# Three operand buffers instead of four in a transformer block's attention: each group's load is issued later

## What is computed

```python
x = x + layernorm(attn(layernorm(x), w_attn, w_proj, adapter_wte, gating))
x = x + layernorm(ffn(layernorm(x), W_gate, W_up, W_down))

# attn: B, T, C = 2, 1024, 512; 32 heads of 16; rotary q and k
q, k, v = split(x @ w_attn.T)
y = softmax(mask(rope(q) @ rope(k).T / 4)) @ v                # causal, 1024 keys
y = y + gating * softmax(q @ adapter_k.T / sqrt(512)) @ adapter_v  # 10 keys
return y @ w_proj.T
# ffn: (silu(x @ W_gate.T) * (x @ W_up.T)) @ W_down.T, width 1376
```

## Time and profile before

| | |
|---|---|
| median of 3 runs | 1271.32 us (1270.86 to 1271.98) |
| the profiled execution, its own time | 1268.47 us |
| its span, first to last instruction | 1266.8 us |
| TensorE busy | 1124.6 us (89%) |
| VectorE busy | 715.8 us (57%) |
| ScalarE busy | 515.2 us (41%) |
| GpSimd busy | 267.5 us (21%) |
| mean granted TensorE clock | 0.932 |
| attention, first maxima matmul to last product | about 232 to 753 us |

### The profile page before, as it was taken

How to read it: one execution, slowest core, us unless ns; L and a number is a source line. 1 busy time by engine, 2 the same in 40 slices (tenths; PEclk the granted TensorE clock), 3 DMA queues, 4 the chain that set the end, 5 groups by cost and what they waited for, 6 DMA issues and landing times. The chain is left out here.

```text
span 1266.8 us, 18587 instructions
## 1 busy us (share of the span) xinstructions
PE 1124.6 (89%) x7036; PEld 766.5 (61%) x7036; DVE 715.8 (57%) x955; ACT 515.2 (41%) x1058; POOL 267.5 (21%) x260
## 2 busy tenths in 40 slices
PE   3999798778999999999999885774999999999996
PEld 1887686433555555555555334663887887887884
DVE  4856645567788788788787015993224324324324
ACT  3224132233777777777777643432111112111111
POOL 3624526300221111112121102662001001001001
PEclk9999998766999999999999777887999999999998
DMA  6356546523444544444440017873000200200200
GB/s 235 104 156 177 132 129 175 122 58 68 77 100 92 96 89 86 78 77 78 79 84 19 21 36 221 282 234 124 1 1 17 84 1 20 82 1 30 70 1 34
DMA packets 82522, 113.10 MB, mean 89 GB/s; under 512 B 24964, under 2 KB 42500, under 8 KB 82436
## 3 DMA queue, kind: packets, MB, share of 16 engines
q1 hardware_dynamic: 80612, 108.22, 33.2%
q10 hardware_dynamic: 1824, 3.70, 1.5%
HBM read 68.83 MB, written 42.21 MB: 88 GB/s over the span
## 5 line engine op out<-in xcount | busy, mean ns | idle before, releaser
L780 ACT ACTIVATE prob<-ps_s 128x512 f32<-128x512 f32 (+3 forms) x768 | 323.2, 496 | 174.1 <-PE ps_s L890 167.2
L802 DVE TENSOR_REDUCE neg<-ps_m 128x2 f32<-128x1024 f32 (+2 forms) x224 | 248.1, 1146 | 66.4 <-PE ps_m L855 37.3
L890 PE MATMUL ps_s<-q_op,k_op 50*128 50x512 f32 (+2 forms) x768 | 248.3, 455 | 26.1 <-ACT prob L780 13.5
L890 PEld LDWEIGHTS ps_s<-q_op,k_op 50*128 50x128 f32 x768 | 121.2, 195 | 130.3 <-ACT prob L780 60.8
L855 PE MATMUL ps_m<-k_op,q_op 48*128 48x512 f32 (+2 forms) x768 | 185.4, 421 | 11.3 <-DVE neg L802 8.3
L755 POOL TENSOR_SCALAR_AFFINE_SELECT prob<-prob 128x512 f32<-128x512 f32 x128 | 81.2, 634 | 432.9 <-ACT prob L780 432.8
L904 PE MATMUL ps_y<-prob,vg 128*17 128x512 f32 (+3 forms) x1536 | 154.8, 524 | 0.0
L1301 DVE TENSOR_TENSOR hf<-sl,ps_u 128x512 f32<-128x512 f32 (+1 forms) x44 | 30.2, 686 | 187.6 <-PE ps_u L74 187.6
L802 DVE TENSOR_REDUCE neg_far<-ps_m 128x4 f32<-128x512 f32 (+2 forms) x96 | 100.4, 1048 | 31.6 <-PE ps_m L860 30.1
L1370 PE MATMUL ps_d<-w_ffn_high,wp_high 128*128 128x512 f32 (+1 forms) x352 | 115.6, 391 | 0.0
L855 PEld LDWEIGHTS ps_m<-k_op,q_op 48*128 48x128 f32 x768 | 96.8, 198 | 30.0 <-DVE neg L802 22.7
(11 more groups left out here) (161 smaller groups left out, 1757.9 us busy)
## 6 DMA issues: line engine op xcount, KB each, us to landing
raw<-in_w_ffn SPq DMA_DIRECT2D x16, 520.0 KB, 5.8
y_heads<-y_sb SPq DMA_DIRECT2D x32, 256.0 KB, 2.1
k_op<-k_parts SPq DMA_DIRECT2D x28, 256.0 KB, 4.4
q_op<-q_parts SPq DMA_DIRECT2D x56, 128.0 KB, 4.9
v_groups<-v_out SPq DMA_DIRECT2D x16, 272.0 KB, 4.0
x<-in_x SPq DMA_DIRECT2D x4, 1024.0 KB, 7.6
q_parts<-part_h SPq DMA_DIRECT2D x16, 256.0 KB, 2.9
q_parts<-part_l SPq DMA_DIRECT2D x16, 256.0 KB, 2.9
```

What stands on the lines that cost most here:

```text
L780: act.activation(prob[:, v % NPROB, h, unit_cols(u)], ps_s[:, y % NS, unit_cols(u)], ACT.Exp, scale=D ** -0.5).then_inc(s_exp, 1)
L802: nc.vector.tensor_reduce(to[:, :, pairs[0]:pairs[-1] + 1, i - TT * c], scores, axis=AX.X, op=ALU.max, negate=True).then_inc(a_read, 1)
L890: nc.tensor.matmul(ps_s[:, y % NS, lo:BLK], k_op[buf][r, pair, j * P:(j + 1) * P], q_op[buf][r, c, pair, lo:BLK], start=True, stop=True)\
```

## The change

One buffer is given up (NBUF is 3), the one on `wqk_l`, with its `vg`. Since group n + 3 now goes into the buffer of group n, a load can be issued only one group later than before: `load(n + NBUF - 1)` is now `load(n + 2)`, in the same place of SyncE's order, and it is left out for n = 0, because group 2 has been loaded ahead of the loop. What it waits for is still the products of group n - 1. GpSimd writes the ones of three buffers instead of four.

```diff
-NBUF = 4
+NBUF = 3
...
-    for i, name in enumerate(("x", "wqk_h", "wqk_l")):
+    for i, name in enumerate(("x", "wqk_h")):
...
         for n in range(NG):
             if n:
                 store_y(n - 1, 1)
-            if n + NBUF - 1 < NG:
+            if n and n + NBUF - 1 < NG:
                 load(n + NBUF - 1)
```

## The result

The changed kernel takes 1434.5 us (four runs, 1432.2 to 1437.5), the kernel before 1271.1 beside it: ratio 1.129, 95% interval 1.126 to 1.131. It is 163 us slower; the forecast was 133, range 1360 to 1440. The span went from 1266.8 to 1430.4 us.

A forecast was written before the change was run, and what follows sets the result against it. TensorE bounds the kernel, busy 27.42 of 28.43 us per attention group. 13 x (5.4 stall - 0.4 won back + 5.2 half clock) = 133 us on 1268.47 gives 1401, plus 2.85: 1404 us, range 1360 to 1440.

The forecast's parts named there:

- The issue, the landing, and the demand 7.85 us behind the store: Load's last DMA issued 6.0 us after the store, landing 6.9 later; TensorE's chunk 0 wants it at 7.85.
- The stall: TensorE waits for the load at chunk 0, 5.4 us (3.7 to 5.9), 13 times without growing or shrinking: 70 us.
- Won back, 0.4: After each stall TensorE regains 0.4 us (0 to 1.0), since ScalarE's exponentials are done and score slots free.
- The clock falls in each stall and rises at the pair of full products: TensorE at half clock from each stall, through 16 steps, to about the end of the pair of full products.
- Its price, 5.2: Half clock costs 5.2 us per group: 3.5 in the 16 steps behind chunk 0, 1.7 in the product pair.
- The rule of the Trainium skill: Half of throttled time is lost: 15.2 us at half clock would cost 7.6, not 5.2; 31 us more in all.
- Per group 5.4 - 0.4 + 5.2 = 10.2 us: Attention groups 1 to 13: stall minus time won back plus half-clock price, 13 times: 133 us.
- from 321.9 to 700.8 TensorE was granted its full clock [...] without a break: Reading of the earlier profile: TensorE at 2.4 GHz (1.00) throughout this stretch of attention.
- Rival 1: Stall at chunk 0 as computed, but the clock stays up or recovers at once: 62 us, 1334; chance 0.11.
- Rival 2: Clock at half for whole groups, stall shrinking to 1.7 us: 17.6 us per group, about 1500; chance 0.04.

The follow-up runs named there:

- Experiment 2: Kernel before with its four buffers, only the load issued one group later, load(n + 2) for load(n + 3): 1435.3 us, ratio 1.124.
- experiment 1: Changed kernel with 48 matmuls of unused result ahead of the wait for the load (the filled groups): 1358.7 us, ratio 1.067.
- experiment 9: Changed kernel, load split between SyncE's queue (ahead of the store) and GpSimd's queue: 1390.2 us, ratio 1.085.
- 12: Kernel of experiment 9 plus 18 matmuls of unused result ahead of chunk 0: 1330.6 us, ratio 1.041.
- experiment 4: Kernel before, four buffers, maxima running less far ahead (LEAD 5 in place of 11): 1329.6 us, ratio 1.045.
- 10: Kernel before, four buffers, with 16 matmuls of unused result ahead of chunk 0 of groups 3 to 15: 1302.8 us, ratio 1.022.
- 11: Kernel before, four buffers, with 48 matmuls of unused result ahead of chunk 0 of groups 3 to 15: 1349.9 us, ratio 1.058.
- experiment 7: Changed kernel, loads of groups 3 to 15 leaving out 6 of their 13 DMAs: 1316.0 us, ratio 1.029.
- experiment 5: Changed kernel, load split between SyncE's queue and ScalarE's, six DMAs issued by ScalarE: 1348.9 us, ratio 1.056.

## Why the prediction was right, and where its sum was short

- *The issue, the landing, and the demand 7.85 us behind the store:* right. The last DMA now took 7.4 us to land in the median, 6.9 before. Experiment 2 shows that nothing else of the change matters.
- *The stall:* said 5.4, measured 5.5 in the mean. It was paid 13 times, between 4.2 and 6.4 us without a trend: right.
- *Won back, 0.4:* wrong, it is 0.1 at most. In group 7 TensorE idles for 41.53 - 34.48 = 7.05 us, 6.12 of it in the stall, so 0.93 us are left where the kernel before has 1.01. In the filled group 33.89 - 32.63 = 1.26 us are idle. ScalarE is ahead after a stall, but TensorE's idle 1.0 us of a group is not where that helps.
- *The clock falls in each stall and rises at the pair of full products:* right. It fell within the stall in each of the 13 groups, and rose within the pair in ten and 0.4 to 0.9 us behind it in three. That idling brings it down, and that this costs the time, is shown by experiment 1, and by 9 against 12. That it is the full products that bring it back is not shown: no run moves them.
- *Its price, 5.2:* right in mechanism, small by 0.5. (158.8 - 71.3 - 8 x 1.6) / 13 = 5.7. From chunk 0 to chunk 0, the stall taken off, the five periods without a short fall are 5.3 to 6.2 us longer than 28.43. The 16 steps took 12.3 us at half clock in group 7 where I had summed 11.7; 0.26 of that is a wait for a score slot that my sum had left out. The pair took 2.8 to 3.6 us, by when the clock rose, where I had 3.5. The rule of the Trainium skill that I weighed ("TensorE: Matmul & The Clock Gate", "HAM oscillation — how this bites in real kernels") has the mechanism, a fall in each tile's wait for its DMA, and the trace agrees, 13 times of 13. By its half of the throttled time the 15.3 us from chunk 0 to the end of the pair would cost 7.6 us, an estimate; the measurement says 5.7.
- *The step that failed:* the sum "Per group 5.4 - 0.4 + 5.2 = 10.2 us", which has no term for a clock that falls where nothing waits. There is a second, short fall in 8 groups, at some 1.6 us each: 13 us, the largest part of what was missing. I had read that "from 321.9 to 700.8 TensorE was granted its full clock [...] without a break" as a property of these steps. Experiments 4, 10 and 11 show that it is none: another order of chunks or another period, with no wait for a load, loses it. What brings a short fall at one turn of the group and not at the next stays open.
- *The rest:* 4.8 us lie outside groups 1 to 13, 3.1 of them ahead of group 1.

The span grew by 163.6 us where the sum has 132.6. The missing 31 us are thus 13 for the short falls, 5 for what was not won back, 7 for the price of the slow steps, 1 for the stall, and 5 outside. All of them point the same way, and 1434.5 lies near the upper end of the range.

Rival 1 (no lasting fall) would have been 1334; with the clock held by work the change costs 84 us, 1355 on the scale of the median before, some 70 of it the matmuls in place of the stall. Rival 2 never occurred: the clock rose again in each group.

## What to carry to other kernels

A buffer is worth the distance between the earliest issue and the demand; read both off the timeline against one common event, here the store, and the stall is a subtraction. A TensorE stall then has a second price that may be as large as itself: look up in the profile what the granted clock did after waits of that length, and count the steps until it rises again. If a stall can't be removed, matmuls without a use in its place can save its second price (76 us of 163 here), and an issue moved to a compute engine's queue has to be priced as a wait of everything that engine feeds.

## What the runs showed of the hardware

- The granted clock fell to 0.50 after waits of 0.5 and 1.9 us in some groups and held after 1.3 in another (experiment 7). In the changed kernel's waits of 4.2 to 6.4 us it fell each time, for 17.1 us, once 20.5.
- It stayed at 0.50 for 14.6 us behind chunk 0 in group 7, through 16 steps in which TensorE idled for 0.3 us.
- It also fell with TensorE busy for 96 to 98% of the group and no load waited for, for 3.4 us and more, where the order of the chunks had changed (experiment 4) or matmuls had been added (10 and 11).
- ScalarE issued a DMA in about 0.45 us and did no exponential meanwhile, 2.3 us for its six (experiment 5); GpSimd's took 0.5 us (experiment 9).
